# Asking for a tile's token rows one tile sooner, and routing the last rows where they already lie

## What is computed

```python
x = layernorm(x + attention(x, wq, wk, wv, wo))      # x: 8 batches x 512 tokens x 512, 16 heads
xt = x.reshape(4096, 512)
logits = clip(xt @ gate_w.T, -50, 50)                # 8 experts
top_w, top_idx = top_k(logits, 2)
rw = softmax(top_w)                                  # two shares per token
# expert e: xt @ (W + scattered entries of e).T, so each token's row is
# rw[0] * xt @ D[top_idx[0]] + rw[1] * xt @ D[top_idx[1]]
out = layernorm(xt + that sum)
```

## Time and profile before

| | |
|---|---|
| median of 3 runs | 1840.94 us (1840.28 to 1843.01) |
| profiled execution | 1839.99 us, its span 1838.2 us |
| TensorE busy | 1776.5 us, 97% of the span |
| DVE, ACT, POOL busy | 1236.2, 814.6, 798.7 us |
| stage of the experts | from about 1552.6 us to the end |
| last matmul ends | about 1804.9 us |

### The profile page before, as it was taken

The page is one execution under the profiler, slowest core; times in us unless marked ns, Lnnn a source line. Parts: engine busy times, 40 slices in busy tenths (PEclk is TensorE's granted clock), DMA queues, the critical chain, the costliest instruction groups (busy, mean ns, idle before and its releaser), DMA issues.

```text
span 1838.2 us, 33411 instructions
## 1 busy us (share of the span) xinstructions
PE 1776.5 (97%) x9290; PEld 1502.2 (82%) x9290; DVE 1236.2 (67%) x3881; ACT 814.6 (44%) x2059; POOL 798.7 (43%) x1092
## 2 busy tenths in 40 slices
PE   8999999999999999999999999999999999999992
PEld 7888888888888888888888888888888887777771
DVE  5566467766777577757775777577766776763256
ACT  4444344434444345534453444444544443333344
POOL 6775445534454333333332333233322334676563
PEclk9999999999999999999999999999999999999996
DMA  9655443335333455454545454544445338545688
GB/s 328 232 216 195 164 141 122 120 99 167 115 116 110 161 160 158 146 174 142 158 147 168 132 159 154 176 146 150 149 143 208 115 126 322 189 167 167 239 312 324
DMA packets 157391, 317.93 MB, mean 173 GB/s; under 512 B 23088, under 2 KB 66256, under 8 KB 146704
## 3 DMA queue, kind: packets, MB, share of 16 engines
q1 hardware_dynamic: 138912, 275.83, 44.6%
q0 software_dynamic: 18288, 39.80, 7.1%
HBM read 227.30 MB, written 88.28 MB: 172 GB/s over the span
## 4 chain that ended last, share of the span: by engine, by line
PE 84%; DVE 4%; issue 4%; DMA 3%; POOL 2%; ACT 2%; DVEq 0%; ACTq 0%; POOLq 0%; SPq 0%
PE psum L1547 23%; PE psum L1549 22%; PE psum L1548 22%; PE psum L1574 7%; PE psum L2309 2%; DMA token_rows<-x,ids_now 2%; PE psum L2311 2%; PE psum L2310 2%; PE psum L372 1%; ACT probs L1824 1%; PE psum L794 1%; DVE pT_lo L1948 1%; POOL expert_weights L1443 1%; POOL probs L1423 0%; POOL expert_slots L649 0%
## 5 line engine op out<-in xcount | busy, mean ns | idle before, releaser
L1423 POOL TENSOR_SCALAR probs<-probs,row_inv 128x128 f32<-128x128 f32 (+3 forms) x512 | 307.9, 625 | 433.0 <-DVE row_inv L1945 431.1
L1824 ACT ACTIVATE probs<-probs,neg_max 128x512 f32<-128x512 f32 (+3 forms) x512 | 282.5, 554 | 360.6 <-DVE neg_max L1937 358.5
L1547 PE MATMUL psum<-xT_hi,w_hi 128*128 128x512 f32 x640 | 252.4, 394 | 0.7 <-DVE qT_lo L1962 0.7
L1937 DVE CUSTOM_DVE_ANT_0 probs<-psum,causal 128x512 f32<-128x512 f32 (+3 forms) x512 | 223.2, 486 | 42.1 <-issue 20.3
L1549 PE MATMUL psum<-xT_hi,w_lo 128*128 128x512 f32 x640 | 250.1, 391 | 0.0
L1548 PE MATMUL psum<-xT_lo,w_hi 128*128 128x512 f32 x640 | 249.7, 390 | 0.0
L1948 DVE TENSOR_TENSOR pT_lo<-psum,pT_hi 128x512 fp32r<-128x512 f32 (+1 forms) x384 | 206.2, 592 | 20.1 <-ACT pT_hi L1834 20.0
L1834 ACT CAST pT_hi<-psum 128x512 fp32r<-128x512 f32 (+1 forms) x384 | 172.3, 526 | 64.9 <-PE psum L1574 64.9
L1547 PE MATMUL psum<-wo_hi,oT_hi 128*128 128x512 f32 x496 | 196.7, 396 | 0.0
L1549 PE MATMUL psum<-wo_hi,oT_lo 128*128 128x512 f32 x496 | 194.1, 391 | 0.0
L1548 PE MATMUL psum<-wo_lo,oT_hi 128*128 128x512 f32 x496 | 193.5, 390 | 0.0
(11 more groups left out here) (251 smaller groups left out, 3866.4 us busy)
## 6 DMA issues: line engine op xcount, KB each, us to landing
w_hi<-split_qk_weights SPq DMA_DIRECT2D x140, 256.0 KB, 2.7
w_lo<-split_qk_weights SPq DMA_DIRECT2D x140, 256.0 KB, 3.0
wo_hi<-split_out_weights SPq DMA_DIRECT2D x27, 1024.0 KB, 5.4
wo_lo<-split_out_weights SPq DMA_DIRECT2D x27, 1024.0 KB, 7.6
expert_weights_hi_lo<-split_expert_weights SPq DMA_DIRECT2D x8, 2048.0 KB, 9.6
x_in<-in_L_attn_x_dram SPq DMA_DIRECT2D x8, 1024.0 KB, 7.5
expert_weights<-fill SPq DMA_DIRECT2D x16, 512.0 KB, 4.3
attn_residual<-y_acc SPq DMA_DIRECT2D x8, 1024.0 KB, 4.7
```

Of the source, the lines that this page charges most:

```text
L1423: last = pool.tensor_scalar(p, p, row_inv[:, buf, i:i + 1], 1.0, ALU.mult, ALU.mult)
L1547: pe.matmul(dst, hi_s, hi_m, start=start, stop=False)
L1824: last = act.activation(probs[:, buf, a:a + w], probs[:, buf, a:a + w], ACT.Exp, bias=neg_max[:, buf, i:i + 1], scale=-1.0, accum_out=row_ ...
L1937: last = dve.tensor_tensor_reduce(probs[:, buf, a:a + w], psum[:, BANK_S + bank, col:col + w], causal[:, T - w:T], -1.0, -MASKED, ALU.add, ...
```

## The change

The fifth tile (tile 4) is fetched by POOL at the end of attention, ahead of `route_place`; `ids_now` of these first five tiles gets a semaphore of its own. In the expert slots POOL fetches tile j + 5, not j + 4, and ACT copies the row numbers of tile j + 6; at the border to tile 33 the copies of 33 and 34 both come in slot 28. The last batch's rows stay in `y_acc`: they are no longer stored to `attn_residual` and loaded again, but normalized and routed in place and written to `x` from there. One scratch tile of the logits moves to the old row buffer, with a wait on the last store from it. Pairs of the second norm start in slot 50 + 2u, not 52 + 2u, and SP waits for the stores of `x` before the first of them is loaded (a buffer of theirs lies over `y_acc`).

```diff
@@ fetch
     if j >= GROUP:
         pool.wait_ge(E.s_turn, j - GROUP + 1)
+    if j <= GROUP:
+        number = pool.value_load(E.tile_number_i[0:1, j:j + 1], min_val=0, max_val=FIRST_COLS - 1)
+        pool.tensor_copy(E.ids_now[:, k:k + 1], E.first_ids[:, bass.ds(number, 1)]).then_inc(E.s_first_ids_now, 1)
+    if j <= GROUP:
+        pool.wait_ge(E.s_first_ids_now, j + 1)
     else:
-        number = pool.value_load(E.tile_number_i[0:1, j:j + 1], min_val=0, max_val=FIRST_COLS - 1)
-        pool.tensor_copy(E.ids_now[:, k:k + 1], E.first_ids[:, bass.ds(number, 1)]).then_inc(E.s_ids_now, 1)
-    pool.wait_ge(E.s_ids_now, j + 1)
+        pool.wait_ge(E.s_ids_now, j - GROUP)
@@ rows_now, route_variance
-    return R.row_bufs[own(tt)]
+    if isinstance(tt, int) and tt >= LAST:
+        return R.y_acc[:, tt - LAST]
+    return R.row_bufs[0][:]
-    dve.wait_ge(*rows_asked(R, tt))
+    if not (isinstance(tt, int) and tt >= LAST):
+        dve.wait_ge(R.s_rows_in, 16 * (tt + 1))
@@ attention, sync
-        sp.wait_ge(s_y_acc, TT + NIT * TT)
-        sp.dma_start(r_store[NB - 1], y_acc[:]).then_inc(s_r_out, 16)
         ready(range(1, NE))
-        sp.wait_ge(s_r_out, 16 * NB)
+        sp.wait_ge(s_r_out, 16 * (NB - 1))
@@ attention, gpsimd
+            if kind == "end":
+                fetch(pool, R, E, GROUP)
             if route:
                 route_place(pool, R, it - TT)
@@ experts
-    FIRST_ROUTED, ROUTE_STEPS, FIRST_PAIR, ... = 3, 5, FIRST_DONE + 5, ...
+    FIRST_ROUTED, ROUTE_STEPS, FIRST_PAIR, ... = 3, 5, FIRST_DONE + 3, ...
+    def ids_of(j):
+        k = j + GROUP + 2
+        if FULL_TILES <= k and j < COUNTED + 2:
+            return ()
+        return tuple(range(FULL_TILES, k + 1)) if j == COUNTED + 2 else (k,) if k < JT else ()
@@ experts, sync
-        ask_rows(LAST)
-        ask_rows(LAST + 1)
         for tt in range(LAST, NT):
             route_store(sp, R, tt, R.x1_dram[tt * P:(tt + 1) * P, :])
-            if tt + 2 < NT:
-                ask_rows(tt + 2)
...
+        sp.wait_ge(R.s_x1_out, 16 * (NT + 1))
         for u in range(Y_BUFS):
             load(u, s_c_in[u])
@@ experts, gpsimd
-            if j + GROUP == FULL_TILES:
+            asked = j + GROUP + 1
+            if asked == FULL_TILES:
                 pool.wait_ge(R.s_x1_out, 16 * (NT + 1))
-            if j + GROUP < JT:
-                fetch(pool, R, E, j + GROUP)
+            if asked < JT:
+                fetch(pool, R, E, asked)
@@ experts, scalar
-            if j + GROUP + 1 < JT:
-                copy_ids(act, E, j + GROUP + 1)
+            for k in ids_of(j):
+                copy_ids(act, E, k)
@@ experts, vector
+        dve.wait_ge(M.s_y_acc, TT + NIT * TT)
+        dve.wait_ge(R.s_x1_out, 16 * (LAST + 1))
         for j in range(1, AHEAD):
             low_tokens(dve, E, psum, j)
```

More of the change, by code:

```diff
@@ L134, in __init__ @@
         self.s_counts, self.s_tables, self.s_step = sem("expert_counts_ready"), sem("tiles_ready"), sem("tables_step")
-        self.s_ids_now, self.s_slot_now = sem("ids_copied"), sem("slots_copied")
+        self.s_first_ids_now, self.s_ids_now, self.s_slot_now = sem("first_ids_copied"), sem("ids_copied"), sem("slots_copied")
         self.s_tok_in = [sem(f"token_rows_{k}_loaded") for k in range(GROUP)]
@@ L474, in __init__ @@
         self.row_bufs = [sb("route_rows", [P, DM])]
-        self.s_late_in = sem("route_late_rows_in")
         self.product = [sb("route_product", [P, DM])]
         self.gate = sb("route_gate", [P, NE, DM])
-def own(tt):
-    return isinstance(tt, int) and tt >= LAST and tt % 2 == 1
 def rows_now(R, tt):
-    return R.row_bufs[own(tt)]
[L489 to L493, removed]
+    if isinstance(tt, int) and tt >= LAST:
+        return R.y_acc[:, tt - LAST]
+    return R.row_bufs[0][:]
 class First:
@@ L580, in build @@
         R.product.append(zone(32 * KB)("route_product_second", [P, DM]))
-        R.product.append(Space(nc, y_at, 4 * DM)("route_product_late", [P, DM]))
-        R.row_bufs.append(Space(nc, y_at + 2 * KB, 4 * DM)("route_rows_late", [P, DM]))
+        R.product.append(Space(nc, rows_at, 4 * DM)("route_product_late", [P, DM]))
+        R.y_acc = y_acc
         late = zone(0, 32 * KB)
@@ L631, in route_store @@
     wait_apart(sp, R.s_x1_ready, tt + 1, R.passed)
-    sp.dma_start(row, rows_now(R, tt)[:]).then_inc(R.s_x1_out, 16)
+    sp.dma_start(row, rows_now(R, tt)).then_inc(R.s_x1_out, 16)
 def route_rstd(pool, R, tt):
@@ L678, in route_variance @@
     dve.wait_ge(R.s_gate_in, 16)
-    dve.wait_ge(*rows_asked(R, tt))
-    dve.bn_stats(R.stats[:], rows_now(R, tt)[:]).then_inc(R.s_stats, 1)
+    if not (isinstance(tt, int) and tt >= LAST):
+        dve.wait_ge(R.s_rows_in, 16 * (tt + 1))
+    dve.bn_stats(R.stats[:], rows_now(R, tt)).then_inc(R.s_stats, 1)
     wait_apart(dve, R.s_stats, 2 * tt + 1, R.passed)
@@ L689, in route_normalize @@
     rows = rows_now(R, tt)
-    dve.tensor_scalar(rows[:], rows[:], R.mean_var[:, 0:1], R.rstd[:], ALU.subtract, ALU.mult).then_inc(R.s_x1_ready, 1)
+    dve.tensor_scalar(rows, rows, R.mean_var[:, 0:1], R.rstd[:], ALU.subtract, ALU.mult).then_inc(R.s_x1_ready, 1)
     dve.wait_ge(R.s_x1_ready, tt + 1)
@@ L697, in route_logits @@
     for e in experts:
-        dve.tensor_tensor_reduce(products[e % len(products)][:], rows_now(R, tt)[:], R.gate[:, e], 1.0, 0.0, ALU.mult, ALU.add,
+        dve.tensor_tensor_reduce(products[e % len(products)][:], rows_now(R, tt), R.gate[:, e], 1.0, 0.0, ALU.mult, ALU.add,
                                  R.logits[:, e:e + 1]).then_inc(R.s_chain, 1)
@@ L2160, in experts @@
     y_pairs = y_dram[0:2 * CAP, :].rearrange("(c u p t) d -> c u p t d", c=2, p=P, t=2)
-    FIRST_ROUTED, ROUTE_STEPS, FIRST_PAIR, PAIR_STEPS, PAIR_END, STORED_LATE, GATED = 3, 5, FIRST_DONE + 5, 2, 6, 4, 3 * GROUP
+    FIRST_ROUTED, ROUTE_STEPS, FIRST_PAIR, PAIR_STEPS, PAIR_END, STORED_LATE, GATED = 3, 5, FIRST_DONE + 3, 2, 6, 4, 3 * GROUP
     COUNTED = FIRST_ROUTED + ROUTE_STEPS * (TT - 1) + 8
@@ L2353, in scalar @@
             high_tokens(act, E, psum, j)
-        copy_ids(act, E, GROUP)
+        copy_ids(act, E, GROUP + 1)
         for j in range(slots_of(JT)):
```

## The result

The changed kernel takes 1835.32 us (median of 7 runs, 1833.46 to 1838.45), the kernel before on the same chip 1842.21 (7 runs, 1840.28 to 1843.97). The forecast was 1829.9, with a range of 1824.0 to 1837.0. The time lies in the range, but only 6.9 of the 11 us came.

A forecast was written before the change was run, and what follows sets the result against it. It took TensorE, busy for 97% of the span, as the bound, with expert-stage stalls above its 3.216 us slot. Gains 6.5 + 0.5 + 1.0 + 3.0 = 11.0 us gave 1829.9 us, range 1824.0 to 1837.0.

The forecast's parts named there:

- A: Expert slots 1 and 2: fetching tile 4 sooner ends TensorE's stall and clock drop, 6.5 us gained.
- R2: Rival, slots 1 and 2: tile 5 comes 2.7 us late, the clock drops again, 2 us gained there, 1834.4 us; chance 0.07.
- DVE keeps its table steps of slots 0 to 3 ... I count nothing for it: First expert slots: DVE's table steps stay and it has no rows to wait for, counted as zero.
- B: Routing stretch and tile 33: sends wait for tile 33's fetch, tile 34 comes about 1 us sooner; 0.5 us gained.
- ACT's cover: Tile 33: tile 27's delayed send still lands before ACT overwrites its buffer, with 2 us to spare.
- The zero for DVE's routing work on other addresses: Routing stretch: DVE does the same work on other addresses, between 0 and 0.3 us either way, taken as 0.
- C: Slots 48 to 67, tokens beside the second norm: a tile more of lead against added traffic, 1.0 us gained.
- R3: Rival, slots 48 to 67: POOL's ring of stores becomes the bound, slower than before, 1846.8 us; chance 0.05.
- a part of the lead turns into a POOL wait: Slots 48 to 67: fetches wait for the store of tile t - 8, sent 4.5 us before, no longer 7.7.
- R1: Rival, slots 48 to 67: sooner pairs add traffic beside the matmuls and bandwidth costs 3.5 us, 1834.4 us; chance 0.18.
- R4: Rival, slots 48 to 67: the tile of lead gains its full 6.5 us, 1824.4 us; chance 0.08.
- D: Behind the last matmul: one pair less and 1.1 MB less to move, 3.0 us gained, bounds 1 and 4.

The follow-up runs named there:

- y3: The kernel before, with only tile 4 fetched at the end of attention, ahead of `route_place`; 1837.07 us, ratio 0.9964.
- x1: The changed kernel, with DVE's two long table steps moved from slots 2 and 3 to slots 4 and 9; 1842.80 us, ratio 0.9986.
- y1: The changed kernel with twelve buffers of slot numbers, not eight, and DVE reading each tile's number one slot sooner; 1818.22 us, ratio 0.9868.
- y4: The changed kernel as it is, run again on the second group's chip; 1837.57 us, ratio 0.9963 against the kernel before.
- x2: The changed kernel with twelve instead of eight buffers of slot numbers, so fetches wait for stores of tile t - 12; 1828.96 us, ratio 0.9913.
- x4: The changed kernel without the lead: tile j + 4 fetched in slot j again, tile 4 still at attention's end; 1838.70 us, ratio 0.9968.
- x3: The changed kernel with pairs of the second norm back at slot 52 + 2u; 1847.13 us, ratio 1.0005.
- z1: The changed kernel with twelve buffers, the number read one slot sooner, and pairs back at slot 52 + 2u; 1833.17 us, ratio 0.9933.
- z3: The changed kernel with twelve buffers, the number read one slot sooner, and pairs from slot 49 + 2u; 1829.17 us, ratio 0.9914.
- z2: The changed kernel, eight buffers kept, with only the tile's number read one slot sooner; 1840.62 us, ratio 0.9981.
- z4: The kernel before, with only the tile's number read one slot sooner; 1844.42 us, ratio 0.9998.

## Why the prediction was right, and where it was not

**A was right in mechanism and size:** 6.6 for 6.5. The clock stayed at its upper level, and tile 5 was not late, so R2 is out. The window of the two slots (columns as in the earlier trace rows):

```profile
1556.00:1562.30 6.30, 6.30 (x34) 5.32 (x33) 4.40 (x25) 2.75 (x6) 4.50 (x6) 1.00 1.02 398
```

**"DVE keeps its table steps of slots 0 to 3 ... I count nothing for it" is the step that failed.** It cost 2.9 us, half of A. The four holes in slots 4 to 6 are where. It was work hidden by the very stall that I removed, and I had priced the stall's end without asking what lay under it, though DVE's rows for slots 2 to 4 were there to be read. y3 shows the loss with the fifth tile alone, and x1 that the waits leave slots 4 and 5 when the steps do. The steps alone do not make it: in y1 they stay, the number is read sooner, and 2.5 us of the loss are gone. It takes the steps and the register load that stands between them and the low part; the load's share is shown on one chip.

**B** gave 0.6 for 0.5: tile 34 no longer waits. POOL stands 5.38 us for the row numbers, as forecast (about 5), tile 33's fetch goes at 1659.55, and ACT's cover held:

```profile
1659.55 0.99 POOL L424 DMA_INDIRECT token_rows<-x,ids_now  x1 [5.38 <-ACT ids_now L407]
```

The zero for DVE's routing work on other addresses seems right: y3, which routes as before, takes as long in slots 3 to 30 (100.4) as y4.

**C: the wrong cause.** I took +1.0 "since it is bandwidth and not lateness that most rows here show"; measured were -1.9, and -1.5 more up to the last matmul (y4: -4.4 in C). x2 shows that it was lateness, made by the ring: the mechanism of R3, to which I gave 0.05 as a whole, and which had its small form in "a part of the lead turns into a POOL wait". R3's own formula was good, its landing not. It asks a landing and 1.3 us of POOL for two tiles. Stores landed in 6.4 us in the median after, not 5.5. That makes (6.4 + 1.3)/2 = 3.85 a tile and 77.0 us for 20, against 75.0 and 77.5 measured. The agreement is rougher than it looks, since only ten fetches waited:

```profile
L2242 POOL DMA_INDIRECT chosen_rows<-y_rows,slot_now x22: 968/985/1446, 1719.3 to 1799.8; - x22
...
DMA to landing us min/median/max: 2.8/6.4/8.4
```

It did not turn the sign, as R3 in full would have, because landings stayed under the 7.0 us that I had named as the point. R1 is refuted as a mechanism: with the ring opened, the same pairs pass beside the matmuls in 65.2 us. Nor does C differ without the lead between pairs from slot 52 (y3, 73.4) and from slot 50 (x4, 73.0, on another chip). R4's 6.5 is what the lead is worth and more, but only with twelve buffers.

The rule that I weighed, the limit of about 358 GB/s in the Trainium skill's page "DMA: Bandwidth & Descriptors" (Specifications), gave 75 us, an estimate, as the least for the stretch of 81.8 us up to the last matmul in which 26.8 MB must pass. (These are not the 20 slots of C, whose 75.03 us in the changed kernel agree with it by chance.) From 0.85 us behind the start of slot 48, as there, to the last matmul the changed kernel takes 85.25 us and moves 26.85 MB at 315 GB/s; x2 takes 73.05 us for 27.1 MB at 371 GB/s, below the 75.6 us that the limit would allow it. Reads and stores are mixed here, and the measurement decides.

**D was right:** 3.4 for 3.0, within its bounds of 1 to 4. x3 against x2 gives 4.5 for two slots, z1 against z3 4.0 to 5.0 for three, of which the third gave nothing.

**The sum.** 6.6 + 0.6 + 3.4 = 10.6 came where forecast (10.0), -2.9 from DVE was not in the sum, -3.3 came in C and up to the last matmul in place of +1.0, and -0.1 in front. With rounding that is the 4.1 of the profiled executions. The medians are 6.9 apart: the profiled execution of before was faster than each of the seven runs beside it, 2.2 us under their median, and that of after 0.5 above its own. The range held, by the width that R1 and R2 gave it, though neither happened. That was luck: it held losses with other causes than those it was widened for. (A small misreading, without effect: in the chain of before the forecast counts four landings of 6.9 us and more; there are five, the fifth of 6.97 us at 1788.24.)

## What to carry to other kernels

When you remove a stall, list what the other engines did under it: that work is uncovered at once, and it is the first term of the loss. A tile of lead is bounded by every ring that the prefetch passes: ask of each how long its slowest user takes to land under load, and lengthen ring and lead together (each alone gave nothing here, both gave 8 to 12 us in C). A high DMA share beside short gaps does not prove that bandwidth is the bound; open the suspected wait and see whether the rate rises.

## What the runs showed of the chip

**Rates.** 370 GB/s at a DMA share of 0.98 held for 65 us (x2), and 398 for 6.3 us in slots 1 and 2.

**A register load is not free.** Where DVE reads a tile's number from memory into a register right ahead of its use, it idles up to 1.1 us, 10.0 us in 20 times in y4. The trace books it as "issue". Read one slot sooner, the idle time is gone in y1; z1, z2 and z3 keep 3.0 to 4.0 us in 3 or 4 times.

**ACT pauses in two of the groups.** In all eight kernels of the first and the third group ACT stands for 2 to 6 us at a time between 1552 and 1710 us, released by nothing that the trace shows ("issue" or "remote"), 35 to 55 us in all. In before, after and the second group it is 1.4 to 3.4 us. From z3, ACT, with TensorE's turn that comes late behind it and DVE between them:

```profile
1627.46 0.69 ACT L2337 ACTIVATE y_rows<-psum,slot_now 128x512 f32<-128x512 f32 x1 [6.09 <-remote]
...
1628.77 0.17 DVE L393 COPY slot_now<-first_slots 128x2 int32 x1 [4.11 <-ACT tokT_hi L380]
...
1629.59 0.66 PE L373 MATMUL psum<-ident,token_rows 128*128 128x128 f32 x4 [0.65 <-DVE tokT_lo L395]
```

ACT's rows of waits between 1552 and 1710 us, x2:

```profile
ACT y_rows L2331 <- remote: 30.3, 8, 5.6
ACT y_rows L2331 <- issue: 13.0, 7, 2.7
```

These kernels take 100.8 to 104.7 us in slots 3 to 30. z1 and z3 run the same instructions there as y1, with the same ring and numbers, and take 103.6 and 102.7 where y1 takes 93.4: 9 to 10 us lie between the groups, not between the kernels. Without the numbers it is 3 us (103.3 to 103.7 in x2, x3 and x4, 100.4 in y4). A DVE that comes 0.5 us sooner helps little where ACT is the late one, which fits z2 and z4. What the numbers are worth beside such pauses is only argued: no kernel without the numbers was profiled in the third group. And what makes the pauses (the chip, or something else that the groups differed in) stays open. The 7 us are shown for the second group's chip alone.
